# Two batches' first accumulators move to other PSUM banks, with a new instruction order on five engines

## The reference, cut to what matters

```python
# layer 0, per batch (non-local block), x: 128 x 256
phi = (w_phi @ x).reshape(c, n); theta = (w_theta @ x).reshape(c, n).T; g = (w_g @ x).reshape(c, n).T
attn = softmax(theta @ phi, axis=1)          # 128 x 128
x = w_mask @ fold(attn @ g) + x
# layer 1 on tokens t = x.T
z = layernorm(t); q, k, v = split(z @ qkv_w.T)          # 8 heads of 16
out = mean over radius 4 and 8 of softmax(masked(q k^T / 4)) v
t = t + out @ proj_w.T + proj_b
# layer 2
t = t + (qdq_fp8(layernorm(t)) @ qdq_fp8(ffn_kernel) + ffn_bias)
```

## Time and profile before

| | us |
|---|---|
| median of 3 runs | 101.0 |
| range of the runs | 100.86 to 103.18 |
| the profiled execution, whole | 100.8 |
| its span, first to last instruction | 99.0 |
| PE, DVE, ACT, POOL busy in it | 91.1, 77.3, 64.3, 57.1 |

### The profile page before, as it was taken

One profiled execution on the slowest core, in us unless ns is written; L12 is line 12 of the kernel. 1 busy time (PEld: TensorE's weight loads), 2 busy tenths in 40 slices (PEclk: granted clock), 3 DMA queues, 4 the chain that ended last, 5 costly groups with the idle time before them and its releaser, 6 DMA issues.

```text
span 99.0 us, 4555 instructions
## 1 busy us (share of the span) xinstructions
PE 91.1 (92%) x1909; PEld 69.8 (71%) x1909; DVE 77.3 (78%) x291; ACT 64.3 (65%) x178; POOL 57.1 (58%) x120
## 2 busy tenths in 40 slices
PE   4999489899999999999999999999999997989990
PEld 3678275794967986976888866978968765666660
DVE  1001625879998799999999999999999899966641
ACT  0535546759677665869865886898678658355450
POOL 5820204321796990858999078592957989940500
PEclk9999999999999999999999999999999999999999
DMA  0644500000000000000001001001001001010110
GB/s 18 180 94 155 190 0 0 7 0 0 10 0 7 7 7 0 7 0 0 7 0 58 1 7 36 27 0 53 6 7 56 3 7 56 0 58 2 57 28 28
DMA packets 4116, 2.91 MB, mean 29 GB/s; under 512 B 960, under 2 KB 4096, under 8 KB 4096
## 3 DMA queue, kind: packets, MB, share of 16 engines
q1 hardware_dynamic: 3872, 2.56, 8.4%
q10 hardware_dynamic: 224, 0.07, 0.3%
HBM read 1.57 MB, written 1.05 MB: 27 GB/s over the span
## 4 chain that ended last, share of the span: by engine, by line
PE 45%; DVE 32%; ACT 9%; issue 8%; POOL 2%; DVEq 0%; POOLq 0%
PE bank L335 10%; PE bank L246 7%; ACT q_four L600 5%; DVE prob_t L872 3%; DVE z_sb L842 3%; PE bank L315 3%; PE bank L358 3%; PE bank L292 2%; DVE v_win L849 2%; PE bank L326 2%; PE bank L319 2%; DVE st L894 2%; DVE t_sb L888 2%; DVE row_max L853 2%; PE bank L373 2%
## 5 line engine op out<-in xcount | busy, mean ns | idle before, releaser
L335 PE MATMUL bank<-k_pad,q_four 64*64 64x64 f32 x512 | 17.1, 220 | 0.2
L335 PEld LDWEIGHTS bank<-k_pad,q_four 64*64 64x64 f32 x512 | 15.7, 135 | 1.8 <-ACT q_four L600 0.9
L1177 POOL TENSOR_TENSOR rstd<-ve,minus_half 128x2 f32<-128x2 f32 x8 | 5.6, 703 | 18.9 <-DVE ve L836 18.9
L246 PE MATMUL bank<-warm_rows 128*128 128x256 bf16 x81 | 13.4, 299 | 1.2 <-DVE warm_rows L770 1.2
L600 ACT ACTIVATE q_four<-bank,four_mask 128x256 f32<-128x256 f32 x32 | 12.6, 484 | 0.0
L350 PEld LDWEIGHTS bank<-prob_t,v_win 32*32 32x32 f32 x1024 | 9.9, 104 | 3.4 <-issue 2.1
L1204 POOL TENSOR_TENSOR prob<-expd,row_inv 128x256 f32<-128x256 f32 x16 | 9.9, 617 | 3.5 <-DVE row_inv L868 3.5
L1198 POOL TENSOR_TENSOR diff<-narrow,row_max 128x192 f32<-128x192 f32 x16 | 8.2, 516 | 6.2 <-DVE row_max L853 6.1
L350 PE MATMUL bank<-prob_t,v_win 32*32 32x32 f32 x1024 | 11.1, 194 | 0.6 <-DVE prob_t L872 0.5
L853 DVE TENSOR_REDUCE row_max<-bank 128x16 f32<-128x512 f32 x16 | 10.6, 666 | 0.8 <-ACT narrow L607 0.8
L612 ACT ACTIVATE expd<-diff 128x448 f32<-128x448 f32 x16 | 9.2, 576 | 2.4 <-POOL diff L1198 1.5
(11 more groups left out here) (117 smaller groups left out, 212.5 us busy)
## 6 DMA issues: line engine op xcount, KB each, us to landing
x_all<-in_x_dram SPq DMA_DIRECT2D x8, 128.0 KB, 3.2
out_dram<-out_all SPq DMA_DIRECT2D x7, 128.0 KB, 2.5
qkv_rows<-in_L_attn_qkv_w_dram SPq DMA_DIRECT2D x1, 192.0 KB, 2.9
out_dram<-out_all SPq DMA_DIRECT2D x2, 64.0 KB, 1.5
proj_rows<-in_L_attn_proj_w_dram SPq DMA_DIRECT2D x1, 64.0 KB, 2.6
ffn_k<-in_L_ffn_kernel_dram SPq DMA_DIRECT2D x1, 64.0 KB, 2.2
proj_bias<-in_L_attn_proj_b_dram SPq DMA_DIRECT2D x1, 64.0 KB, 3.7
theta_w<-in_L_conv_w_theta_dram SPq DMA_DIRECT2D x1, 32.0 KB, 2.0
```

Of the source, the lines that this page charges most:

```text
L246: mm(bank[at][:, 0:TOK], warm_rows[:, 0:C], warm_rows[:, :], start=True, stop=True)
L335: last = mm(ps_scores[g][q, w, :, :], q_four[q, u % SLOTS, g * WB + w, :, :].rearrange("p e q -> p (e q)"), k_pad[q, u % SLOTS, at:at + KW ...
```

## The change

Batches 1 and 3 (`GUEST`) take banks 6 and 7 in place of 0 and 1. The waits follow: each batch waits for the batch before it in the same pair of banks, so `apply_bilinear(1)` and `project_g(1)` wait for none, batch 2 waits for batch 0, batch 3 for 1, batch 4 for batch 2, and from batch 5 on all is as before. `weigh_values(0, 0)` now also waits for `e_done` of 4 batches, `turn_t2(0)` for `z_done` of 4. The folded weight moves from bank 6 to 4 and the filler from bank 7 to 5. No computing instruction is added or removed, except that the filler goes from 23 to 22 before the first batch's work is through, and from 58 to 60 at the end.

The lists of PE, ACT, DVE and POOL are written in a new order. The core of the diff:

```diff
+GUEST = (1, 3,)
...
+        def first_bank(u):
+            return bank[6] if u in GUEST else bank[0]
+
+        def second_bank(u):
+            return bank[7] if u in GUEST else bank[1]
+
+        def batches_before(u):
+            same = [p for p in range(u) if (p in GUEST) == (u in GUEST)]
+            return same[-1] + 1 if same else 0
...
-                wait(pe, e_done, u)
-                mm(ps_u, bilinear_t[:, :], x_all[:, u, :], start=True, stop=True).then_inc(u_mm, 1)
+                wait(pe, e_done, batches_before(u))
+                mm(first_bank(u)[:, 0:TOK], bilinear_t[:, :], x_all[:, u, :], start=True, stop=True).then_inc(u_mm, 1)
...
-                wait(pe, z_done, u)
+                wait(pe, z_done, batches_before(u))
...
             def weigh_values(u, g):
+                if u == 0 and g == 0:
+                    pe.wait_ge(e_done, GUEST[-1] + 1)
...
             def turn_t2(u, s=None):
+                if u == 0:
+                    pe.wait_ge(z_done, GUEST[-1] + 1)
```

More of the change, by code:

```diff
@@ L952, in _ @@
+            band_max(0, 0)
+            norm_first(2)
+            subtract_max(0, 0)
+            window_values(1)
+            band_max(0, 1)
+            subtract_max(0, 1)
+            row_sums(0, 0)
             row_inverse(0, 0)
+            column_max(5)
+            column_inverse(4)
+            stats_first(3)
             row_sums(0, 1)
-            norm_first(2)
             row_inverse(0, 1)
+            aggregate_first(3)
+            turn_probs(0, 0)
             band_max(1, 1)
+            band_max(1, 0)
@@ L957, in _ @@
+            subtract_max(1, 0)
+            variance_first(3)
             subtract_max(1, 1)
-            band_max(1, 0)
-            column_inverse(3)
-            turn_probs(0, 0)
-            subtract_max(1, 0)
+            stats_first(4)
+            column_inverse(5)
+            turn_probs(0, 1)
+            aggregate_first(4)
+            row_sums(1, 0)
+            norm_first(3)
+            row_inverse(1, 0)
+            pick_odd(0)
+            variance_first(4)
+            window_values(2)
@@ L991, in _ @@
-            norm_first(4)
+            row_sums(2, 0)
             pick_odd(1)
-            variance_second(0)
+            row_inverse(2, 0)
+            band_max(3, 0)
             window_values(3)
+            subtract_max(3, 0)
             band_max(3, 1)
-            row_sums(2, 0)
-            column_inverse(5)
+            turn_probs(2, 0)
+            residual(1)
+            quantise_tiny(0)
             subtract_max(3, 1)
-            row_inverse(2, 0)
+            stats_first(5)
+            quantise_half(0)
@@ L1009, in _ @@
-            quantise_half(0)
-            variance_first(5)
-            column_max(6)
-            stats_second(1)
-            row_sums(3, 0)
-            turn_probs(2, 0)
+            norm_first(5)
+            pick_odd(2)
             row_inverse(3, 0)
+            window_values(4)
+            band_max(4, 0)
+            subtract_max(4, 0)
             band_max(4, 1)
-            column_inverse(6)
-            norm_first(5)
+            turn_probs(3, 0)
             subtract_max(4, 1)
-            aggregate_second(1)
@@ L1122, in _ @@
             aggregate_second(7, 0)
-            pick_odd(7, 1)
             variance_second(7, 0)
```

530 lines of the change are left out of this document (253 added, 277 removed).

## The result

| | before | changed |
|---|---|---|
| median of 4 runs each | 101.1 us | 98.19 us |
| range | 100.86 to 103.18 | 97.77 to 98.78 |
| the profiled execution | 100.8 | 98.29 |
| its span | 99.0 | 96.6 |

The ratio is 0.9724, with a 95% interval of 0.9658 to 0.9791. In two later groups of runs, each beside runs of the kernel before, the same changed kernel came to 0.9793 [0.9750, 0.9837] and 0.9789 [0.9740, 0.9839]. So the change is worth 2.1 to 2.8%, some 2.1 to 2.8 us. Executions at a lower clock, or over 1.5% above the fastest of their kernel, occur with all these kernels and are left out of all ratios; where they pull a median up, the text goes by the ratio.

A forecast was written before the change was run, and what follows sets the result against it. A head that waits, a middle with PE and VectorE both full, and a tail bound the kernel. VectorE's lead 2.85, less 0.3 (middle) and 0.4 (tail), gives 2.1 us off 100.8: 98.7 us, own range 98.0 to 99.3, overall 97.2 to 100.6.

The forecast's parts named there:

- PE's head: Up to the first scores: scores(0, 0) at about 19.1, 0.4 us later with 2.56 us more done; PE 2.2 us ahead.
- VectorE's head: Up to band_max(2, 0), forecast at 34.25 us with 2.7 us more work done: VectorE 2.85 us ahead at 34 us.
- The middle: Stretch with PE and VectorE both full: lead kept but not grown, 0.3 us lost; bounds 0 and 1.5 us.
- The tail: From row_sums(7, 0) to the last result: 14.0 us instead of 15.0, a loss of 0.4; bounds 0 and 1.4.
- the filler on PE: In the tail: two more fillers, 0.2 us on PE where it idles anyway.
- The sum: Whole kernel: 2.85 - 0.3 - 0.4 = 2.1 us gained from 100.8, giving 98.7 us.
- the lead "stays": In the middle: the same work goes through the same two full engines, so the lead stays but does not grow.
- the rival called slower: In each batch lay_mask waits for subtract_max, PE's and VectorE's lists lock: about 102.8 us; chance 0.08, 0.05 over 2%.
- the rival that only the head's bank waits go: Head: 2.1 us of waits go, x[2] returns 0.6; 1.5 us less the tail, 99.7 us; chance 0.3 shared with another rival.

The follow-up runs named there:

- its early place: Changed kernel with the load of x[2] issued right behind that of x[1], ahead of the weights' loads: 97.65 us, ratio 0.9693; again 97.85 us, 0.9701.
- the swap: Changed kernel with batch 7's first half put ahead of batch 6's last layer on ScalarE, PE and VectorE: 98.43 us, ratio 0.9756.
- Banks alone: Kernel before, all engines in their old order, with batches 1 and 3 in banks 6 and 7 and the matching waits: ratio 1.0054.
- the early join: Kernel before with VectorE's quantise_join moved right behind quantise_parts, ahead of band_max(0, 0): ratio 1.0025.
- the new head and the old rest: New banks and new order up to the first softmax, then the kernel before's order on all engines, less work already done: ratio 0.9996.

## Why the prediction was right

The forecast was 98.7 us and the median came to 98.19, inside the forecast's own range of 98.0 to 99.3. Point by point:

- **PE's head.** Right in its course. `apply_bilinear(2)` waited for x[2] and not for a bank. The load took from 6.54 to 10.22 us by the chain of waits, 3.7 us instead of 3.5, and `column_attention(1)` ended at 9.0, so PE waited 1.3 us where 0.6 were forecast (at its early place the same load took 2.3 us). `scores(0, 0)` came at 19.56 instead of 19.1, with the 2.56 us of work ahead. PE's lead was 1.7 us, not 2.2.
- **VectorE's head.** `norm_first(1)` came at 17.29 (17.4), `band_max(0, 0)` at 21.11 (21.5), `band_max(2, 0)` at 34.50 (34.25). The join was mis-sized: it took 1.15 us at its new place, not 1.69, with nothing but a power of 128x2 elements beside it on GpSimd. At the price of its old place the lead at `band_max(2, 0)` is 2.7 - 0.1 = 2.6 us, against 2.85.
- **The middle.** This term had the wrong sign. Forecast was a loss of 0.3 us. By the prediction's accounts the stretch should have taken 47.57 - 2.7 + 1.4 = 46.3 us without any loss; it took 45.44 us. That is 0.8 us better (45.42 and 45.93 us in the two later traces of the same kernel, so 0.4 to 0.9). VectorE's idle time fell from 0.83 to 0.46 us. The rest is shorter busy time. The means of one `y_tiny` and one `y_half` fell from 418 to 394 and from 414 to 390 ns, those of `z_sb`, `out_all` and `prob_t` by 6 to 14 ns, which makes some 0.4 us in the stretch; no run tells why.
- **The tail.** Forecast 14.0 us from `row_sums(7, 0)`, measured 94.60 - 79.94 = 14.66; the loss is 1.4 - 0.4 = 1.0 us instead of 0.4. The term that was put at nothing is the filler on PE, "where it idles anyway". Batch 6's last layer does come early: its power starts 4.23 us behind the mark, against 5.67 before. All operands of `feed_forward(6)` are ready at 87.97 us, when `y_half` ends, but PE starts it at 88.80. The chain of waits shows what stands between, the seven fillers of `keep_warm(0, 7)`, with a pause in their middle:

```profile
87.56 0.41 DVE L927 TENSOR_SCALAR y_half<-bank 128x256 fp8e4<-128x256 f32 x1
```

```profile
87.24 0.33 PE bank L256 x3
87.57 0.79 issue
88.35 0.61 PE bank L256 x4
88.96 0.11 PE bank L395
```

`project(7, 1)`, the next call, then starts at 89.13, although its input was ready at 88.42, and the second half's `residual` comes 9.79 us behind the mark against 10.16 before: 0.4 us earlier where 1.0 were forecast. An estimate from these rows: without the pause `project(7, 1)` would start at about 88.5 and that `residual`, 0.6 us behind it, at 9.2 us, which is the forecast. All nine traces with this tail have the pause behind the third filler, 0.62 to 1.05 us long, and the swap's has it with 0.29; the four with the old tail have none in that place. The code has no wait between the fillers, and no row says what PE waits for, so its cause stays open. No run took the fillers out.

- **The sum.** 2.6 + 0.8 - 1.0 = 2.4 us, against 2.85 - 0.3 - 0.4 = 2.1. The mechanism of the head is right and near in size. That the total comes so close is partly luck: the middle was 1.1 us better than forecast, the lead and the tail together 0.9 us worse. The two later medians of the same kernel, 98.64 and 98.95 us, lie near the forecast, too.

**What the experiments took from the reasoning.** The prediction said that the lead "stays" in a middle with the same work. With the old middle it does not: there PE's part of it was gone by 32 us, and at the end, behind the old tail, all of it. So it needs a rewritten order behind the head. The mechanism of the rival called slower, `lay_mask` behind `subtract_max`, is what eats it there, 1.3 us at the first instance. And the rival that only the head's bank waits go is refuted from both sides. Banks alone bring nothing to the time, and the whole brings more than that rival's 1.5 us less the tail.

What stays open: why the middle got 0.8 us shorter than its work, what the new middle does without the new head, and what makes PE pause in the tail. No run took the old tail with the new head and middle.

## What to carry to other kernels

When two engines are full in the same stretch, price a change by what it takes from both; in the old order here, the time of a call taken from only one of them turned into idle time. A wait for a buffer may be the visible wait and still be worth nothing: look at the next call in the same engine's list and ask what that one waits for. And when work is pulled forward, look at once for the transfer that feeds it: here the load's place in the queue, on which no engine waited before, became worth about 1 us. And look in the chain for stretches that no engine released: the largest error of this forecast's tail was a pause in matmuls that have no use of their own but stand ahead of one that has.

## What the runs showed of the hardware

VectorE's copies of 128x128 from f32 to bf16 take 0.22 to 0.23 us with GpSimd idle (the early join's trace) and 0.52 to 0.79 us beside GpSimd additions of 128x256. Beside GpSimd's power on 128x2 elements, which lasts 0.75 us, the copy stayed at 0.23 us:

```profile
19.63 0.75 POOL L1189 TENSOR_TENSOR rstd<-ve,minus_half 128x2 f32<-128x2 f32 x1 [2.68 <-DVE ve L848]
...
20.11 0.23 DVE L822 CAST kq<-k_part 128x128 bf16<-128x128 f32 x1
```

The loads of x[0] and x[1], 128 KB each, with loads of 0.5 to 192 KB issued behind them, landed in 2.3 to 2.5 us. The load of x[2] took 3.5 to 3.7 us with the other five of its size behind it at steps of 0.48 us, and 2.3 us at its early place.

In the kernel with only batch 3 as guest PE was busy for 0.81 of 2.00 us from 12 to 14 us, and its granted clock was 0.50 from 16 to 18 us. With the banks alone PE was busy for 0.47 of 2.00 us from 12 to 14 us, and the clock stayed at 1.00 up to 20 us. So these rows do not tell what the clock goes by.

PE can pause within a row of equal matmuls that wait for nothing in the code: 0.79 us in the tail of the changed kernel, 1.53 us at 41.3 us in the kernel with the new head and the old rest, both at a granted clock of 1.00.
